# A graph layer in one kernel: the first norm applied in halves, the third tile's statistics moved ahead of a weight slice, and the norm's finish moved ahead of the remainders

## The reference

```python
xn = _layernorm(x, axis=-1)                       # x: 1250 x 1024, f32
x = x + gnn(xn, edges, W, b) + mix(xn, Wq, bq, Wk, bk, Wv, bv, Wo, bo)
x = x + ffn(_layernorm(x, axis=-1), w1, w2, h1, h2, w3)
# gnn: relu(segment_sum((xn @ W)[src] * norm) + b), 41,250 edges
# mix: linear attention, 16 heads: K, V, Q = xn @ W.T + b, phi = elu + 1,
#      S = phi(K).T V, Z = sum phi(K), out = (phi(Q) S / (phi(Q) Z + eps)) @ Wo.T + bo
# ffn: silu(x w1) * (x w2) -> gelu(h1) -> gelu(h2) -> w3
```

## Time and profile before

| | |
|---|---|
| Time, median of 3 runs | 1004.16 us (1002.57 to 1004.26) |
| The profiled execution | 1000.12 us, span 998.3 us |
| PE busy | 974.8 us, 98% |
| DVE busy | 544.0 us, 54% |
| ACT busy | 293.7 us, 29% |
| POOL busy | 142.3 us, 14% |

### The profile page before, as it was taken

The page is one execution under the profiler, slowest core; times in us unless marked ns, Lnnn a source line. Parts: engine busy times, 40 slices in busy tenths (PEclk is TensorE's granted clock), DMA queues, the critical chain, the costliest instruction groups (busy, mean ns, idle before and its releaser), DMA issues.

```text
span 998.3 us, 13321 instructions
## 1 busy us (share of the span) xinstructions
PE 974.8 (98%) x4860; PEld 824.2 (83%) x4860; DVE 544.0 (54%) x1067; ACT 293.7 (29%) x584; POOL 142.3 (14%) x191
## 2 busy tenths in 40 slices
PE   4999999999999999999999999999999999999998
PEld 3887888888889989978786788767788999999986
DVE  5986769669644788782113556446556312122354
ACT  5873214123223343241212222113113312135300
POOL 7101001001011050050300000000301203064100
PEclk9999999999999999999999999999999999999999
DMA  7413103103011022122201466535521402010053
GB/s 267 161 38 89 29 18 115 28 18 112 15 47 53 26 79 83 52 68 95 93 15 55 144 199 177 160 116 171 183 80 73 139 1 85 1 43 1 22 186 141
DMA packets 46979, 86.78 MB, mean 87 GB/s; under 512 B 19036, under 2 KB 23388, under 8 KB 46896
## 3 DMA queue, kind: packets, MB, share of 16 engines
q1 hardware_dynamic: 38416, 57.28, 17.7%
q0 software_dynamic: 8480, 28.45, 8.8%
HBM read 61.62 MB, written 24.09 MB: 86 GB/s over the span
## 4 chain that ended last, share of the span: by engine, by line
PE 90%; DVE 5%; ACT 2%; DMA 1%; issue 1%; POOL 1%; SPq 0%; DVEq 0%; ACTq 0%; POOLq 0%
PE PS L1417 11%; PE PS L1419 10%; PE PS L1418 10%; PE PS L1539 9%; PE PS L1538 9%; PE PS L1540 9%; PE PS L1596 5%; PE PS L1598 4%; PE PS L1616 3%; PE PS L1617 3%; PE PS L1615 3%; PE PS L1457 2%; PE PS L1669 2%; PE PS L1668 2%; PE PS L1667 2%; PE PS L1432 2%
## 5 line engine op out<-in xcount | busy, mean ns | idle before, releaser
L1417 PE MATMUL PS<-ring,act_t 128*128 128x512 f32 (+1 forms) x480 | 194.3, 405 | 1.3 <-POOL ring L438 0.6
L1419 PE MATMUL PS<-ring,act_t 128*128 128x512 f32 (+1 forms) x480 | 190.2, 396 | 0.0
L1418 PE MATMUL PS<-ring,act_t 128*128 128x512 f32 (+1 forms) x480 | 190.0, 396 | 0.0
L1538 PE MATMUL PS<-act_t,ring 128*128 128x416 f32 (+1 forms) x432 | 159.4, 369 | 1.4 <-POOL ring L438 1.3
L1539 PE MATMUL PS<-act_t,ring 128*128 128x416 f32 (+1 forms) x432 | 152.3, 353 | 0.0
L1540 PE MATMUL PS<-act_t,ring 128*128 128x416 f32 (+1 forms) x432 | 151.8, 351 | 0.0
L1417 PEld LDWEIGHTS PS<-ring,act_t 128*128 128x128 f32 (+1 forms) x480 | 89.6, 187 | 24.1 <-POOL ring L438 1.6
L1419 PEld LDWEIGHTS PS<-ring,act_t 128*128 128x128 f32 (+1 forms) x480 | 89.3, 186 | 22.2
L1418 PEld LDWEIGHTS PS<-ring,act_t 128*128 128x128 f32 (+1 forms) x480 | 89.6, 187 | 21.0 <-issue 0.5
L1538 PEld LDWEIGHTS PS<-act_t,ring 128*128 128x128 f32 x432 | 81.4, 188 | 6.8 <-issue 3.4
L1539 PEld LDWEIGHTS PS<-act_t,ring 128*128 128x128 f32 x432 | 81.5, 189 | 4.0 <-issue 3.4
(11 more groups left out here) (194 smaller groups left out, 1651.5 us busy)
## 6 DMA issues: line engine op xcount, KB each, us to landing
stage_x<-in_wslices_dram POOLq DMA_DIRECT2D x54, 256.0 KB, 4.2
stage<-in_wslices_dram POOLq DMA_DIRECT2D x42, 256.0 KB, 3.8
xr<-x_d SPq DMA_DIRECT2D x18, 512.0 KB, 3.6
phin_d<-phiq SPq DMA_DIRECT2D x8, 625.0 KB, 3.1
xrow<-in_x_dram SPq DMA_DIRECT2D x9, 512.0 KB, 3.6
xh<-in_x_dram SPq DMA_DIRECT2D x18, 256.0 KB
x_d<-xh SPq DMA_DIRECT2D x18, 256.0 KB
x_d<-xr SPq DMA_DIRECT2D x9, 512.0 KB, 3.2
```

The costliest lines, as they stand in the source:

```text
L1417: pe.matmul(out_ap, node_rows(0, k, t), ring[:, slot(k0 + k), 0, :], start=(k == 0), stop=False)
L1418: pe.matmul(out_ap, node_rows(1, k, t), ring[:, slot(k0 + k), 0, :], start=False, stop=False)
L1419: ins = pe.matmul(out_ap, node_rows(0, k, t), ring[:, slot(k0 + k), 1, :], start=False, stop=(k == KD - 1))
L1538: pe.matmul(out_ap, w[0], x_t[:, 0, k, o:o + n], start=(k == 0), stop=False)
```

## The change

Five edits, the last two of which concern the mixing stage:

- `ln_apply(0)` is done in two halves of 512 columns. The first raises a new semaphore `xn_first`, and the first four transposes wait only for that one. On ACT it stands behind `hi(0)` alone, where it stood behind `hi(0)` and `hi(1)`; `transposed_hi(0)` comes ahead of `hi(2)` and `hi(3)`.
- `ln_stats(2)` and `ln_finish(2)` stand earlier on DVE: the statistics ahead of the remainder of slice 7, the finish ahead of `transposed_lo(1)`. On ACT, `ln_root(2)` stands ahead of `hi(8)` and `hi(9)`.
- PE transposes tile 1 after five pieces of the first product, where it was four.
- In mixing, `ln_finish` stands ahead of `transposed_lo`.
- For i >= 10 the transposes of every second tile go into PSUM banks 3 and 4 (`tr_bank`), and a tile's transposes wait for the remainders of the tile before the last.

```diff
+        def tr_bank(i):
+
+            return 3 if i >= NT and i % 2 else 5
...
+                if i == 0:
+                    nc.scalar.activation(to[:, 0:512], of[:, 0:512], ACT.Identity, bias=ln[0:r, 0, 5:6],
+                                         scale=ln[0:r, 0, 4:5]).then_inc(xn_first, 1)
+                    to, of = to[:, 512:D], of[:, 512:D]
                 nc.scalar.activation(to, of, ACT.Identity, bias=ln[0:r, i % 2, 5:6],
                                      scale=ln[0:r, i % 2, 4:5]).then_inc(xn_ready, 1)
...
             ln_root(0)
             hi(0)
+            ln_apply(0)
             hi(1)
-            ln_apply(0)
+            transposed_hi(0)
             hi(2)
             hi(3)
-            transposed_hi(0)
             ln_root(1)
             hi(4)
             hi(5)
             ln_apply(1)
-            for n in range(6, 10):
-                hi(n)
+            hi(6)
+            hi(7)
+            ln_root(2)
+            hi(8)
+            hi(9)
             for step in range(40):
                 r = rows(step % NT)
                 if step < 9:
                     transposed_hi(step + 1)
-                if step == 0:
-                    ln_root(2)
...
             ln_finish(1)
-            for n in LO_FIRST[1:]:
-                weight_lo(dve, n)
+            weight_lo(dve, LO_FIRST[1])
             dve.wait_ge(x_in[0], 32)
             ln_stats(2)
+            weight_lo(dve, LO_FIRST[2])
+            ln_finish(2)
...
                 if step < 9:
                     transposed_lo(step + 1)
-                if step == 0:
-                    ln_finish(2)
...
                 ln_stats(NT + j)
+                ln_finish(NT + j)
                 if 1 <= j < NT - 1:
                     transposed_lo(NT + j - 1)
-                ln_finish(NT + j)
...
-                pe.wait_ge(xn_ready, i + 1)
-                if i >= 1:
-                    pe.wait_ge(tr_lo, 2 * i)
+                if i:
+                    pe.wait_ge(xn_ready, i + 1)
+                    pe.wait_ge(tr_lo, 2 * i if i <= NT else 2 * (i - 1))
+                if i == NT + 1:
+                    pe.wait_ge(den_read, 24)
                 for g in range(2):
+                    if i == 0:
+                        pe.wait_ge(xn_ready if g else xn_first, 1)
...
-                    if fresh and t == 0 and k == 4:
+                    if fresh and t == 0 and k == 5:
                         transpose_tile(1)
```

More of the change, by code:

```diff
@@ L285, in build @@
         std_ready = sem("std_ready")
+        xn_first = sem("xn_first")
         rstd_ready = sem("rstd_ready")
@@ L728, in transposed_hi @@
                         act_t[:, 0, 4 * g:4 * g + 4, t * P:t * P + rows(t)],
-                        PS[:, 5 + g, :].rearrange("p (a b) -> p a b", a=4)[:, :, 0:rows(t)],
+                        PS[:, tr_bank(i) + g, :].rearrange("p (a b) -> p a b", a=4)[:, :, 0:rows(t)],
                         ACT.Copy).then_inc(tr_hi, 1)
@@ L1392, in transpose_tile @@
                 src = xn if i < NT else xn2
-                pe.wait_ge(xn_ready, i + 1)
-                if i >= 1:
-                    pe.wait_ge(tr_lo, 2 * i)
+                if i:
[3 more added lines that the diff above has]
+                    pe.wait_ge(den_read, 24)
                 for g in range(2):
+                    if i == 0:
+                        pe.wait_ge(xn_ready if g else xn_first, 1)
                     for j in range(4):
                         e = 4 * g + j
-                        ins = pe.transpose(PS[:, 5 + g, j * P:j * P + r], src[0:r, i % 2, e * P:(e + 1) * P],
+                        ins = pe.transpose(PS[:, tr_bank(i) + g, j * P:j * P + r], src[0:r, i % 2, e * P:(e + 1) * P],
                                            ident[0:r, 0:r])
```

## The result

The changed kernel takes 996.84 us (median of 6 runs, 995.55 to 997.37), the kernel before 1003.23 us (6 runs, 1002.34 to 1004.26; three of them are those that the prediction started from). The ratio is 0.9941, with a 95% interval of 0.9926 to 0.9955: 5.9 us faster (the medians are 6.4 apart). The forecast was 1000.6 us, with a range of 998.9 to 1002.9. The sign was right, the size was not: the time lies 2.1 us under the range.

What follows compares the result with a forecast made beforehand. PE, busy 98% of the span, bounds the kernel, so only its waits for the norm's apply count. Start 1.9 plus mixing 1.7 make 3.6 us: profiled 1000.12 to 996.5, with 4.0 carried 1000.6; range 998.9 to 1002.9.

Steps and rivals of the forecast that it cites:

- the carrying of one execution to the median: Whole kernel: profiled execution 1000.12 goes to 996.5; its 4.0 below the median of 1004.16 is kept, giving 1000.6 us.
- The start, 1.9 us: Steps 1 to 4: transposes of tile 2 at 22.05 instead of 23.81, those of tile 5 at 43.0 instead of 44.89.
- Halves: Norm of tile 0: first transposes 1.1 us earlier, at 8.4, but slice 3's remainder and the chain to tile 2 0.3 later.
- The load of tile 2: Start, DVE: statistics of tile 2 wait for their load, landing at 16.7, 7.3 us after issue; at most 0.5 earlier.
- rival A: Start: load lands 0.5 us earlier with its issue, phik isn't held; total gain 4.0 to 4.5, 999.7 to 1000.2; chance 0.18.
- ACT's list: Start: slice and PSUM copies queued behind the root, not DVE, set the start of tile 2's apply, near 20.8.
- What becomes of it: Step 0: POOL's slice 8 holds phik until 25.7 instead of 27.59; DVE 1.9 us ahead, passed on to tiles 3 to 5.
- Mixing, 1.7 us: Mixing, j = 1: finish first lets PE transpose at 687.3 instead of 688.98; 0.3 of the 2.00 wait stays.
- the banks at zero: Mixing: banks 3 and 4 are free since the denominators; waiting for the tile before costs nothing.
- B: Start gives nothing: phik held by slices 8 and 9, ending at 27.6; only mixing's 1.7 us left, 1002.5; chance 0.16.
- C: No change to speak of: mixing's 2.00 wait turns into another and the start gives nothing; 1004 us; chance 0.08.
- D: Steps 0 and 1: new pauses keep PE's clock slow, 41 matmuls 0.2 longer each; 2.6 us slower, 1006.8; chance 0.04.

Runs made afterwards that it cites:

- the last job: Changed kernel without the halves (tile 1 transposed after four pieces), and the changed kernel again, against the kernel before: both 0.9950, medians 996.24 and 996.49 us.

## Why the prediction was off

**The failed step is the carrying of one execution to the median**: "it was 4.0 below the median of 1004.16, and I carry the same difference". The changed kernel was worked out at 996.5 for an execution like the profiled one, and its timed median is 996.84; nearly all of the error is the 4.0 that was added. They were not a constant. The median of the three runs lay 0.9 above that of the six, and the rest is PE's clock, which the profiled execution had at full speed behind its start and most timed ones had not. So a term was missing, put at nothing because one trace showed no fall: what the clock costs behind the two pauses.

The mean spans give it. At a clock of 1.000 the kernel before has 998.3 (7 executions) and the changed one 994.7 (7 executions): 3.5 us, and 3.6 had been worked out. The mean of all executions lies 2.2 above that before (1000.5) and 0.1 after (994.8), so the missing term is 2.1 us. The two make 5.7, against the 5.9 of the ratio. The clock's bounds, 3.1 less 0.5, would give 2.7, which is more than the spans show. The size moves with the runs: in the last job, where both kernels ran on one chip, the same two differences are 3.7 and 1.5 (998.5 and 999.9 before, 994.8 and 994.7 after).

**The start, 1.9 us.** Right. Transposes of tile 5 at 42.96 from 44.89: 1.93.

- Halves: a loss on the chain, not a gain, as forecast. Slice 3's remainder came 0.7 later than before (13.41) where 0.3 was forecast; 0.2 of that is a later first load, and the half apply took 0.8, not 0.6 (the second half too, which ended at 9.42, not 8.9). The first transposes came at 8.86, not 8.4.
- The load of tile 2 sets the statistics: forecast 16.75, measured 16.66, with a wait of 0.34. It took 7.2 to land. The issue was at 9.45, no earlier than before, since the two halves together ended when the whole had; so whether an earlier request lands earlier, as rival A wanted, was not tried.
- ACT's list sets the apply: forecast 20.8, measured 20.66.
- What becomes of it: DVE was forecast to be held by POOL's slice 8 until 25.7. It was, but one instruction later. DVE and POOL, changed kernel:

```profile
24.08 0.41 DVE L1159 SCALAR_TENSOR_TENSOR phik<-kb,kexp 128x256 f32<-128x256 f32 x1
24.40 1.34 POOL L443 TENSOR_TENSOR ring<-stage_x,ring 128x512 fp32r<-128x512 f32 x1
24.53 1.37 DVE L1164 COPY ksum<-phik 128x256 f32<-128x256 f32 x1
```

phik ran freely, and the copy behind it took 1.37, ending 0.16 behind POOL's instruction; the same copy took 0.29 in the execution of before. The finish of tile 3 began at 25.93; the forecast's 25.7 and the 0.36 from phik's end to the finish in the trace of before give 26.06. The Trainium skill, "SBUF — State Buffer", "Who interferes with whom", has the one issued first keep the shared interface, and has copies among the operations that can take it. This execution agrees on both points, with 24.08 against 24.40; the one before, in which phik started first by the trace and was held, does not agree on the order.

**Mixing, 1.7 us.** Right in the profile (1.69 from L966 to the apply, 0.33 left), and the banks at zero were right. In the timed runs the part alone is worth 2 to 3 us; the part above 1.7 is put down to the clock, whose bound fell by 0.6 to 1.2 us.

One gain was given back in the profiled execution: ahead of mixing PE waited 1.42 for a remainder (L1592) where it had waited 0.7. This wait was between 0.2 and 2.3 us in the twelve further profiles, with and without the change, and is taken to be part of the spread of the runs.

**The rivals.** A (the load lands earlier) did not happen: what fell below 1000 was for another reason. (Its upper end is also too high by its own steps: 2.6 and 1.7 make 4.3, not 4.5.) B and C did not happen. D, a slower clock, was the right resource with the wrong sign. I ruled a fall behind the pauses out because "after 3.64 us of idleness at 23.81 the trace shows no return to the slow level". That was one execution, and not a typical one. The rule of the Trainium skill that I set beside it ("TensorE: Matmul & The Clock Gate", "HAM oscillation — how this bites in real kernels": a long enough pause lets the clock fall) was shown by the very next profiled execution of the same kernel, behind 3.20 us; I had noted that by it the change "could only help", gave it no price and no chance, and it was worth 2.1 us.

Of D one sign did come: matmuls of 0.63 went on past 14.4, to 17.1 (the row at 16.64). It didn't bring D's loss, and it isn't the change's doing. The end of this first slow stretch moves from execution to execution, from about 14.7 to 18 in the 14 profiles, and in the kernel before, repeated, it came at 16.1. It sets how long PE then waits ahead of tile 2, since the transposes there come when `xn` does: with the start as before and these transposes at 23.7 to 23.9, PE waited 3.64, 3.20 and 2.23 us as the slow stretch ended at about 15, 16 and 18. With the start's edits alone it ended at 14.7 and the wait was 1.79; in the changed kernel it ended at 17.1 and the wait was 1.17.

What stays open: why filling the first pause alone raised the mean clock but not the speed, what decides in which execution a pause is followed by a fall, how the 2.1 us divide between the start and mixing, and whether the halves cost half a microsecond.

## What to carry to other kernels

Before one profiled execution is used as the baseline, set its time beside all timed runs. If it is at their fast edge, find out what it lacks; here the list of mean clocks per run would have told it. A pause of PE has two prices, its length and the slow matmuls behind it in part of the executions, so price a shortened pause with both. And when a step is moved earlier, look at what it will then wait for (here a load) and at whose list sets the next start (here ACT's copies): that part of the forecast held to 0.15 us.

## What the runs showed of the hardware

- The same program has its clock fall in one execution and not in the next. In the 14 profiled executions, 16 pauses of PE at the three places (ahead of tile 2, ahead of mixing, in mixing) were between 1.8 and 4.1 us long; behind 10 of them the clock fell, behind the shorter ones at these places never. Length alone doesn't decide: it fell behind 1.79 (the kernel without the banks) and not behind 3.64 (the kernel before). Once (the kernel with nine filling matmuls) it also fell, from about 369 to 372 us, behind waits of 0.57 and 0.74, which the other 13 have too.
- A fall behind a pause of 3.2 us or more at the start lasted 6.8 us (three profiles), one behind 1.8 to 2.3 us, wherever it was, 3.4 (seven falls). The clock can also fall while PE stands still, where it costs nothing (behind the last matmul of the changed kernel).
- The granted clock reads 1.00 at the start of the program, while the first matmuls take 0.63 us and not 0.39; when that ends differs by about 3 us between executions.
- A DVE copy of 128 x 256 f32 that takes 0.29 us took 1.37 beside a GpSimd subtraction that had started 0.13 before it.
